# Attention over a fixed graph: O's two halves are added ahead of its transposition, two heads are turned at once, and the loop body is doubled

## The reference

```python
h = maximum(layernorm(x), 0.0)
q = (h @ Wq + bq).reshape(b, n, H, HD)      # k, v alike
scores = einsum('bihd,bjhd->bhij', q, k) / sqrt(HD)
mask = where(adj == 0, -1e9, 0.0)
weights = softmax(scores + mask, axis=-1)
out = einsum('bhij,bjhd->bihd', weights, v)
return x + out.reshape(b, n, H * HD)
```

## Time and profile before

| | |
|---|---|
| median of 3 runs | 4149.26 us (4145.04 to 4152.58) |
| the profiled execution | 4145.39 us, of which the span is 4143.3 us |
| busy shares | PE 98%, PEld 81%, ACT 76%, DVE 75%, POOL 32% |
| granted TensorE clock | 0.999 on average |

### The profile page before, as it was taken

One profiled execution on the slowest core, in us unless ns is written; L12 is line 12 of the kernel. 1 busy time (PEld: TensorE's weight loads), 2 busy tenths in 40 slices (PEclk: granted clock), 3 DMA queues, 4 the chain that ended last, 5 costly groups with the idle time before them and its releaser, 6 DMA issues.

```text
span 4143.3 us, 77847 instructions
## 1 busy us (share of the span) xinstructions
PE 4075.5 (98%) x22528; PEld 3339.6 (81%) x22528; DVE 3111.1 (75%) x5128; ACT 3142.6 (76%) x5642; POOL 1313.3 (32%) x1665
## 2 busy tenths in 40 slices
PE   7999999999999999999999999999999999999999
PEld 6888888888888888888888888888888888888887
DVE  6877868778677786777767677786877768767687
ACT  5877868778687786877868688686886868868687
POOL 4333332333323333333333233332333333333222
PEclk9999999999999999999999999999999999999999
DMA  5221212212122221222212122121221212212111
GB/s 178 72 75 57 82 46 78 67 57 82 57 68 67 60 85 60 59 68 75 69 60 68 59 77 67 60 77 49 77 67 60 80 47 77 73 54 85 47 52 31
DMA packets 219597, 282.56 MB, mean 68 GB/s; under 512 B 12304, under 2 KB 143376, under 8 KB 210576
## 3 DMA queue, kind: packets, MB, share of 16 engines
q1 hardware_dynamic: 219152, 277.14, 22.2%
HBM read 172.23 MB, written 37.75 MB: 51 GB/s over the span
## 4 chain that ended last, share of the span: by engine, by line
PE 92%; ACT 2%; issue 2%; DMA 2%; POOL 1%; DVE 1%; SPq 0%; POOLq 0%; ACTq 0%; DVEq 0%
PE T L528 20%; PE misc L486 17%; PE S L516 11%; PE S L517 11%; PE O L540 10%; PE O L547 10%; PE misc L499 8%; PE misc L555 3%; DMA xln<-in_x 2%; PE misc L465 1%; ACT yparts L636 1%; ACT probs L653 1%; ACT pT L645 0%; DVE pT L811 0%; DVE bn L769 0%
## 5 line engine op out<-in xcount | busy, mean ns | idle before, releaser
L811 DVE TENSOR_TENSOR pT<-T,pT 128x512 fp32r<-128x512 f32 x2048 | 1401.5, 687 | 758.4 <-ACT pT L645 745.7
L645 ACT CAST pT<-T 128x512 fp32r<-128x512 f32 x2048 | 1189.0, 592 | 654.2 <-PE T L528 553.4
L805 DVE CUSTOM_DVE_ANT_0 S<-S,mask 128x1024 f32<-128x1024 f32 x1024 | 1257.4, 1228 | 10.0 <-issue 4.9
L528 PEld LDWEIGHTS T<-ident,probs 128*128 128x128 f32 x8192 | 1012.5, 140 | 270.1 <-ACT probs L653 14.1
L528 PE MATMUL T<-ident,probs 128*128 128x128 f32 x8192 | 1226.3, 272 | 3.7 <-DVE pT L811 2.9
L653 ACT ACTIVATE probs<-S,negmax 128x1024 f32<-128x1024 f32 x1024 | 1151.1, 1124 | 8.9 <-DVE negmax L805 5.8
L547 PE MATMUL O<-pT,vs 128*64 128x512 f32 x2048 | 975.6, 476 | 0.2 <-DVE pT L811 0.2
L540 PE MATMUL O<-pT,vs 128*128 128x512 f32 x2048 | 817.5, 399 | 14.0 <-issue 13.9
L486 PE MATMUL misc<-hT,wqk 128*128 128x512 f32 x3036 | 788.4, 395 | 8.1 <-ACT yparts L636 7.7
L486 PEld LDWEIGHTS misc<-hT,wqk 128*128 128x128 f32 x3036 | 557.0, 188 | 158.8 <-issue 25.7
L403 POOL TENSOR_TENSOR yparts<-yparts 128x256 f32<-128x256 f32 x256 | 188.3, 736 | 1112.4 <-ACT yparts L636 1112.4
(11 more groups left out here) (70 smaller groups left out, 3703.3 us busy)
## 6 DMA issues: line engine op xcount, KB each, us to landing
wqk<-wqk_split SPq DMA_DIRECT2D x63, 1024.0 KB, 7.0
xln<-in_x SPq DMA_DIRECT2D x240, 256.0 KB, 4.2
xres<-in_x SPq DMA_DIRECT2D x66, 512.0 KB, 3.7
kA<-kA SPq DMA_DIRECT2D x128, 256.0 KB, 3.2
kB<-kB SPq DMA_DIRECT2D x128, 256.0 KB, 3.8
out<-xres SPq DMA_DIRECT2D x64, 512.0 KB, 3.2
probs<-in_adj SPq DMA_DIRECT2D x4, 1024.0 KB, 4.9
wqk_split<-vs SPq DMA_DIRECT2D x3, 1024.0 KB, 10.5
```

Source lines behind the costliest of these rows:

```text
L528: mm = pe.transpose(T[:, u % 2, i * P:(i + 1) * P], probs[:, (GB * g + i) % RING, j * P:(j + 1) * P], ident[:])
L645: act.copy(pT[:, u % PT, 0, :], T[:, u % 2, :]).then_inc(p_hi, 1)
L805: dve.tensor_tensor_reduce(S[:, s % 2, :], S[:, s % 2, :], mask[:, s % NB, :], 1.0, 3.0e38, ALU.add, ALU.min, negmax[:, s % RING:s % RING ...
L811: dve.tensor_tensor(pT[:, u % PT, 1, :], T[:, u % 2, :], pT[:, u % PT, 0, :].bitcast(F32), ALU.subtract).then_inc(p_lo, 1)
```

## The change

Instead of being transposed, the halves of O are now brought together first. SP copies one half of `oT`'s rows to the other partitions (`move_o`, slots 2, 10, 18, 26 of a pair), POOL adds the other half to it (`sum_o`, slots 5, 13, 21, 29 of a pair) into `oP`, whose rows 0 to 63 then hold one head of the pair and rows 64 to 127 the other. One `turn_out` then serves both heads: it runs in slots 2 and 10 of the next pair only. ACT's `copy_y` and POOL's `finish` (now two operations of 128x512) run as often. `copy_out` waits for `sum_o` of the group before, where it waited for `turn_out`. x's residual tile has one buffer instead of two, stored and loaded in slot 12 of a pair. The x tiles are normalised and turned in slots 71, 77, 80, 83, 87, 91, 94, 97; the statistics of all eight are in the first two pairs. The loop has 7 rounds of two samples instead of 14 of one.

```diff
-HT_SLOTS = (83, 85, 87, 88, 91, 92, 95, 96)
+HT_SLOTS = (71, 77, 80, 83, 87, 91, 94, 97)
...
-STATS_SLOTS = ((5, 7, 13), (37, 39, 45), (69, 71))
+STATS_SLOTS = (5, 7, 11, 13, 37, 39, 43, 45)
...
+STORE_AT, COPY_K_AT, WQK_AT = 12, (8, 15), 16
+OUT_AT = (2, 10)
+PER = UNITS // PAIRS
...
+            def move_o(b, g):
+                n, half, second = GROUPS * b + g, g % 2, (g // 2) % 2
+                sp.wait_ge(o_copied, n + 1)
+                sp.sem_inc(sp_passed)
+                used = 2 * (PAIRS * b + g // 4) + half - 1
+                if some(used):
+                    sp.wait_ge(o_turned, used)
+                    sp.sem_inc(sp_passed)
+                own, other = (slice(0, HD), slice(HD, P))[::-1 if second else 1]
+                sp.dma_start(oP[own, half, :], oT[other, :]).then_inc(o_moved, 16)
...
+                    if u % NB == LAG and not (first and u == LAG):
+                        if u == LAG:
+                            move_o(b - 1, GROUPS - 1)
+                        else:
+                            move_o(b, u // NB - 1)
+                    if v == STORE_AT and not (first and p == 0):
+                        sp.wait_ge(y_added, 2 * (PAIRS * b + p))
...
+                    if u in HT_AT and HT_AT[u] + XLN < NB and not last:
+                        t = HT_AT[u]
+                        sp.wait_ge(h_turned, NB * (b + 1) + t + 1)
+                        load_xln(b + 1, t + XLN)
+                    if v == WQK_AT and not (last and p >= PAIRS - 2):
...
+            with sp.Fori(0, B // 2 - 1) as two:
+                body(2 * two + 1)
+                body(2 * two + 2)
...
+            def sum_o(b, g, last=False):
...
+                gp.wait_ge(o_moved, 16 * (n + 1))
+                gp.tensor_tensor(oP[rows, half, :], oP[rows, half, :], oT[rows, :], ALU.add).then_inc(o_summed, 1)
...
+                gp.tensor_tensor(y[:], y[:], rinv[:, half].unsqueeze(3).to_broadcast([P, GB, 2, HD]),
                                  ALU.mult).then_inc(y_scaled, 1)
...
-            def turn_out(b, g, free):
-                pe.wait_ge(o_copied, GROUPS * b + g + 1)
+            def turn_out(b, p, half, free):
+                pe.wait_ge(o_summed, GROUPS * b + 4 * p + 2 + half + 1)
                 pe.wait_ge(*free)
...
-                        if u > LAG:
-                            turn_out(b, u // NB - 1, before(b, u, True, last))
+                        if u >= PER and u % PER in OUT_AT:
+                            turn_out(b, u // PER - 1, OUT_AT.index(u % PER), before(b, u, True, last))
...
                 if some(n):
-                    act.wait_ge(o_turned, n)
+                    act.wait_ge(o_summed, n)
                 act.copy(oT[:], O[:]).then_inc(o_copied, 1)
```

More of the change, by code:

```diff
@@ L327, in body @@
-                    if not (last and p >= PAIRS - 2):
+                        sp.wait_ge(stored, 16 * (PAIRS * b + p))
+                        load_xres(b, p)
+                    if u in STATS_AT and not last:
+                        t = STATS_AT[u]
+                        sp.wait_ge(bn_done, NB * (b + 1) + t + 1)
+                        load_xln(b + 1, (t + XLN) % NB)
+                    for half in range(2):
+                        if v == COPY_K_AT[half] and not (last and p == PAIRS - 1):
+                            copy_k(b, p + 1, half)
@@ L433, in body @@
                 for u in range(UNITS):
+                    if u % NB == LAG + 3 and not (first and u == LAG + 3):
+                        if u == LAG + 3:
+                            sum_o(b - 1, GROUPS - 1)
+                        else:
+                            sum_o(b, u // NB - 1, last)
                     if u in STATS_AT and not last:
@@ L612, in _ @@
             body(0, first=True)
-            with pe.Fori(1, B - 1) as b:
-                body(b)
+            with pe.Fori(0, B // 2 - 1) as two:
+                body(2 * two + 1)
+                body(2 * two + 2)
             body(B - 1, last=True)
@@ L618, in _ @@
                 contract_lo(B - 1, u)
-            turn_out(B - 1, GROUPS - 1, (y_copied, GROUPS * B - 1))
+            for half in range(2):
+                turn_out(B - 1, PAIRS - 1, half, (y_copied, 2 * (PAIRS * B - 1) + half))
         @block.scalar
@@ L753, in _ @@
             body(0, first=True)
-            with act.Fori(1, B - 1) as b:
-                body(b)
+            with act.Fori(0, B // 2 - 1) as two:
+                body(2 * two + 1)
+                body(2 * two + 2)
             body(B - 1, last=True)
             copy_out(B - 1, GROUPS - 1)
-            copy_y(B - 1, GROUPS - 1)
+            for half in range(2):
+                copy_y(B - 1, PAIRS - 1, half)
         @block.vector
@@ L884, in _ @@
             body(0, first=True)
-            with dve.Fori(1, B - 1) as b:
-                body(b)
+            with dve.Fori(0, B // 2 - 1) as two:
+                body(2 * two + 1)
+                body(2 * two + 2)
             body(B - 1, last=True)
```

159 lines of the change are left out of this document (71 added, 88 removed).

## The result

The changed kernel takes 4212.7 us (median of 4 runs, 4210.2 to 4222.0) against 4149.8 before (4 runs): ratio 1.0158, 95% interval 1.0145 to 1.0171. It is slower by 63 us, where the prediction said 4168, 19 slower, and 4205 at most. The profiled execution has a span of 4210.7 us against 4143.3, 67.4 more, and a granted clock of 0.993 on average against 0.999.

The account below looks back on a forecast made before the run. It took the kernel to be bound by PE's instruction chain, with ACT and DVE nearly bounding by latency. Terms -45 - 9 + 29 + 19 + 6 + 5 + 14 = +19 us gave 4164 profiled, 4168 median; 8-in-10 range 4105 to 4205.

Parts of the forecast that it names:

- The removal of the turns: 128 turns of O removed; a plain slot (no projection) gives 0.34 us, slots 90 and 122 more: -45 us.
- rival 3: ACT and DVE can't follow a faster PE, so the six plain slots give nothing: 4195 us, chance 0.10.
- Slots 78 to 88: Third pair: PE waits in slot 87 for tile 4, behind a sum of O queued behind the weights; 18.4 against 16.5: +29 us.
- the late sums: `copy_out` of slot 25 waits for a late `sum_o` in the first two pairs and slightly in the fourth: +19 us.
- the end: After the last contraction, the sum stands behind the first half's finish, followed by turn, copy and POOL again: +5 us.
- the clock: Behind the standstill in slot 87 the clock falls in 8 of 15 samples, losing half of 3.4 us: +14 us.
- The K copies, which need 3.2 alone, ... start 0.5 to 0.8 later in the queue: First two pairs: store and load of x delay K's copies, hence the weights and O's half; priced within +19 us.
- The tiles turned in slots 71 and 77 follow a projection: PE's weight load behind a projection waits for ACT, taken as 0.15 us twice; part of +6 us.
- slot 98: The turn of O there, behind the tile of slot 97, waits 0.1 us; part of +6 us.
- the loop ends: With 7 rounds instead of 14, PE has 6 back edges instead of 13, saving 1.3 us each: -9 us.
- Rival 2: O's half does not wait behind the weights, landing in about 3 us: -66, 4083 us; chance 0.20 with its like.

Follow-up runs that it names:

- turns_cut: Kernel before with three of the four transpositions of O left out in slots 18 and 26 of each pair: 4118.4 us, ratio 0.9924.
- wqk_late: Changed kernel with the 1 MB of weights issued in slot 20 of a pair instead of 16, behind O's half: 4131.8 us, ratio 0.9948.
- filled_wait: Changed kernel with 24 transpositions of the identity into the free PSUM bank ahead of tile 4's turn in slot 87: 4190.6 us, ratio 1.0101.
- changed_head: Changed kernel with 16 transpositions of the identity on PE ahead of everything: 4211.7 us, ratio 1.0153.
- store_late: Changed kernel with the store and load of x's residual tile issued in slot 28 of a pair instead of 12: 4187.3 us, ratio 1.0091.
- both_late: Changed kernel with the weights issued in slot 20 of a pair and the store and load of x in slot 28: 4103.4 us, ratio 0.9890.
- tile_71: Changed kernel with weights in slot 20 and tiles turned in slots 77, 79, 81, 84, 87, 91, 94, 97: 4141.9 us, ratio 0.9977.
- spread: Changed kernel with store and load of x in slot 28, weights in 22, tiles in slots 77, 79, 83, 85, 88, 91, 94, 97: 4109.4 us, ratio 0.9903.
- later_tile: As spread, with the fourth tile turned in slot 86 instead of 85: 4095.4 us, ratio 0.9868.
- before_doubled: Kernel before with only the loop body doubled, 7 rounds of two samples: 4135.8 us, ratio 0.9965.
- one_sample_loop: Changed kernel with the loop of before, 14 rounds of one sample: 4249.8 us, ratio 1.0234.
- body_pad: one_sample_loop with 40 matmuls of 4 columns in slot 54 of its body: 4493.7 us, ratio 1.0838.
- one_sample_pad: one_sample_loop with 64 small matmuls of 4 columns ahead of everything on PE: 4285.8 us, ratio 1.0316.

## Why the prediction was too low

The direction and most steps were right; the sum was 48 us too low, and 45 us are stalls that it has no term for.

**Right.** The removal of the turns: 0.39 a plain slot (slot 18 -0.44, slot 19 +0.05) where 0.34 was taken, since slot 19 took 0.05 back and not the 0.1 that was allowed for. turns_cut shows the same without the rest of the change; rival 3 is out. Slots 78 to 88, the late sums (by wqk_late 17 us), the end, and the clock (filled_wait: 15.4 us, the prediction 14) came within 3 us each. Some of that closeness is luck. The terms of the stretch add up to 18.3 and not 18.35. The clock fell behind slot 87 in 11 of 15 samples, where 8 were taken, but cost 1.4 us each and not 1.7; in changed_head, with the same wait, it fell in 14, and in store_late in 9.
The Trainium skill (TensorE: Matmul & The Clock Gate, Part 1) puts the fall behind a time without work. Taken strictly that means no fall here, since PE still worked 0.61 of the 3.41 us; the clock fell in 11 samples, and the measurement decides. The direction agrees: filled_wait, with work in the same gap, has no fall there.

**Failed: "The K copies, which need 3.2 alone, ... start 0.5 to 0.8 later in the queue".** Two things were wrong in it. The delay was mis-sized: the second copies of the first pair land 2.0 us later from their issue than before (median 5.7 against 3.7, and 4.5 to 7.5 in samples 1 to 14). And it was priced for O's half alone and not for the copies' own reader, PE's first score of the next pair, which now waits 1.1 us a sample in slot 22 and 0.6 in slot 54, 26 us in all. With 0.8 us more than before, the copy of sample 4 would have landed at 11.3 us behind slot 14's turn, ahead of the score at 11.7 (11.67 in the samples without a wait), so it is the size that made the stall. store_late and both_late show the queue as its cause. The prediction had asked who waits for O's half, and had not asked it for K's copies in the same queue.

**Failed: "The tiles turned in slots 71 and 77 follow a projection", 0.15 each.** It looked at what stands ahead of the tile and not behind it, and so put the wait behind it at nothing. The wait ahead is 0.1; behind it the projection of slot 72 waits 1.3 us, since between the turn and it PE has one slot, and ACT and DVE have two chunks of copies in that time. tile_71, spread and later_tile give 19 us for it, and later_tile shows that the tiles can be packed closer behind slot 77 if their loads are in time. The same in small is slot 98, 0.4 a sample instead of 0.1.

**Mis-sized: the loop ends, -9.** The term is right for the kernel before (before_doubled, 9.1 in the slots) and wrong for the changed one, -2: the changed code has a second stall behind each jump back. Without the doubling the change would have cost 37 us more (one_sample_loop). The rows of before don't show it: that kernel has no such stall, single or doubled (before_doubled: 0.4 us at that line), and changed_head loses it by a shift alone.

**Rival 2** was wrong as to the queue, and right as to what a kernel without that queue gives: 15.0 us for the stretch. wqk_late is 49 us above its 4083; slots 22, 54 and 72 alone are 56, and smaller differences take some back.

Three things stay open. That a loop end costs up to 2.9 us a round in one place and 1.1 in another is tied to the blocks by their number alone; I did not find which instruction must lie where, and 16, 32 and 48 transpositions all did it. Why the landing of K's copies varies from sample to sample (slot 22 grew by 0 to 3.4 us) is not shown. Nor is why the clock falls in some samples behind the same wait and not in others.

## What to carry to other kernels

A change that moves transfers is priced queue by queue: for each one that now lands later, look up its reader, also where the transfer itself wasn't touched. A sum that waits for a DMA should be the last and not the first in an in-order engine's slot: here one exchange of two instructions was worth 72 us, 1.7%, and moving three DMA issues (the weights, and the store and load of x) to later slots 109 us. When a loop body changes size, look at the idle by issue at its ends; a few instructions in an idle time ahead of the loop may be worth 0.5%, and two kernels that differ in nothing else can differ by that much.

## What the runs showed of the hardware

Shifting a loop of PE by 32 instructions took 21 us from 4095 (0.5%), with no other change, and left two blocks of instructions to load around each end instead of four; in one_sample_loop PE idled 2.9 us at each end, in before_doubled 1.1. A standstill of PE of about 3 us cost more than itself: 15.4 us over the 11 samples in which the clock fell, another 1.4 each. The clock also fell without a standstill: in body_pad it went to 0.50 for 10 to 20 us in slot 54 of every sample, while PE worked without a gap through the 40 small matmuls. A float32 matmul of 128x4 was not cheap: each of the 64 in one_sample_pad is two in the trace, with a weight load each, and the 128 took 27.47 us, 0.21 each, at the start of the execution:

```profile
1.57 27.47 PE L610 MATMUL T<-ident 128*128 128x4 f32 x128 [1.57 <-POOL ident L357]
```
